# Routed blocks of the second feed-forward as three products of rounded parts, with the parts of the weights made in the first

## The chip, the core and the metric

The kernel runs on one core of a Trainium2 chip. The metric is the time of one execution on the device, in microseconds (us); lower is better. Several executions are timed and their median is given; one more is recorded by the hardware profiler. The core has five engines with an instruction stream each: PE (TensorE, the matrix array, fed by a sequencer of its own), DVE (VectorE), ACT (ScalarE), POOL (GpSimd) and SP (SyncE, which here only starts transfers). They wait for each other through semaphores.

## The reference

```python
def _layernorm(x, axis=-1, eps=1e-05): ...
x = L0_attn_x                                   # 8 x 512 x 256 float32
x = x + 0.5 * ffn(_layernorm(x), ...)
x = x + attention(_layernorm(x), ...)           # 16 heads of 16, causal
x = x + 0.5 * ffn(_layernorm(x), ...)           # same weights as the first

def ffn(x, router_w, expert_bias, shared_w1, shared_w2, shared_w3, routed_w1, routed_w2, routed_w3):
    shared_out = silu(x @ shared_w1) * (x @ shared_w2) @ shared_w3      # hidden width 1024
    scores = sigmoid(x @ router_w)                                      # 16 experts
    _, top_idx = top_k(scores + expert_bias, 2)
    gates = scores of the two chosen experts, 0 for the others
    for each expert e:                                                  # hidden width 256
        acc = acc + silu(x @ routed_w1[e]) * (x @ routed_w2[e]) @ routed_w3[e] * gates[:, e]
    return shared_out + acc
```

All is float32. The bias makes the choice of experts uneven. Running this reference's own arithmetic on its inputs gives, for the second feed-forward, these 128-row blocks for each of the 16 experts in turn: 26, 3, 27, 1, 2, 0, 0, 3, 0, 0, 0, 0, 4, 0, 2, 0 (68 blocks with rows in them).

## The kernel before

The stages follow one another: `norm_first`, `feed_forward` (tag f1_), `attention`, `feed_forward` (tag f2_). The same function serves both feed-forwards; the argument `fill` is true for the first alone.

**The shared part.** 4096 rows are taken in 8 chunks of 512. Five chunks (`BEHIND` = 5) run before the routed blocks (`chunks_before`) and three after (`chunks_behind`). Here each float32 operand is already kept as a rounded high part and a low part (type float32r), and a product is three matmuls of parts: high by high, high by low, low by high (lines 943, 959, 963). Meanwhile DVE works out the routing, SP loads the 16 experts' weights (`load_expert`, tile f_ew: ew12 and ew3), and POOL scatters the rows into `rows_by_slot`, sorted by expert into 128-row blocks.

**The routed blocks.** There are always NB = 80 blocks, each with one expert; `bexp_i` holds the expert's number of each, and blocks beyond the last used one take expert 15. `steps` lets every engine walk through steps i = 0 to 81; in step i PE (function `step` under `block.tensor`) does this in order: read the number of block i's expert from SBUF into a register (`value_load`, L998), two plain float32 matmuls 128x512 with that expert's w1 and w2 (L1007), the two transposes of the hidden rows of block i-1 (L1015), the two transposes of the input rows of block i+1 (`turn_x`, L994), read the expert's number of block i-2 again, and its two float32 matmuls 128x256 with w3 (L1028). Weight addresses depend on the register, so each matmul with an expert's weights needs one address instruction on PE's sequencer (FUSED_REGOPS). ACT copies the turned input out of PSUM (L654) and takes silu (L647); DVE multiplies (L897), copies the turned hidden rows (L894) and the result (L904); POOL scatters the result to `outputs_by_choice` (L612); SP fetches the next block's rows, four blocks ahead (L491). The loop is rolled: 4 steps written out, 6 turns of 12, then 6 more steps.

The order on each engine is the order in which the code is written. A wait on PE's sequencer holds everything written behind it on PE.

Of the kernel before, what the change touches and what calls it, by code (L numbers as in the profile page):

```python
# [6 lines left out]
P = 128  # L7
F32 = mybir.dt.float32
# [8 lines left out]
CT = 4  # L17
# [26 lines left out]
class Mem:  # L44
# [8 lines left out]
    def ps(self, name, shape, dt=F32):  # L53
        return self.ctx.enter_context(self.nc.psum_tensor(self.tag + name, shape, dt))

# [224 lines left out]
def feed_forward(nc, z, g, dram, tag, x_src, fill, out):  # L280
# [11 lines left out]
    BEHIND = NC - 3  # L292
    with ExitStack() as ctx:  # L293
        m = Mem(nc, ctx, tag)
        ew12 = m.sb("ew12", [P, E, KD, 2 * RH])
        ew3 = m.sb("ew3", [P, E, KR, z.D])
        ewf = ew12[:].rearrange("p e k n -> p (e k n)")
# [15 lines left out]
        rawx = m.sb("rawx", [P, KD, CHUNK])  # L313
        xparts = m.sb("xparts", [P, 2, 2, KD, CHUNK], F32R)
        xr = m.sb("xr", [P, 2, CT, z.D])
        sil = m.sb("sil", [P, 2, CHUNK])
        hid = m.sb("hid", [P, 2, CHUNK])
        hparts = m.sb("hparts", [P, 2, 2, CHUNK], F32R)
# [8 lines left out]
        bexp_i = m.sb("bexp_i", [1, NB], I32)  # L327
# [3 lines left out]
        xq = m.sb("xq", [P, 4, CT // 2, z.D])  # L331

        bcmp = early([NB, E])[0:1]

# [3 lines left out]
        far0 = E * KD * 2 * RH - 2 * (IN_A + IN_B) - 4 * NT * TOPK - 2 * NB  # L338
        assert used[0] <= far0
        far_experts = E - -(-(E * KD * 2 * RH - far0) // (KD * 2 * RH))  # L340
# [14 lines left out]
        yr = xq[:, 0:2].rearrange("p u t d -> p (u t) d")  # L355
        assert used[0] <= E * KD * 2 * RH and KD * CHUNK == 4 * z.D and CHUNK == 2 * RH
# [58 lines left out]
        mid = m.sem("mid")  # L415
        summed = m.sem("summed")
# [8 lines left out]
        def steps(eng, body):  # L425

            for r in range(4):
                body(0, r, lambda lag, n=r: 0 <= n - lag < NB)

            assert (NB // 4 - 2) % 3 == 0  # L430
            with eng.Fori(0, (NB // 4 - 2) // 3) as turn:
                for part in range(3):
                    for r in range(4):
                        body(turn * 3 + (part + 1), r, lambda lag: True)
            for n in range(NB - 4, LAST + 1):
                body(n // 4, n % 4, lambda lag, n=n: 0 <= n - lag < NB)
# [17 lines left out]
        def _(sp):  # L454
# [28 lines left out]
            def load_expert(e):  # L483
                for dst, src in ((ew12[:, e, :, 0:RH], dram.routed_w1), (ew12[:, e, :, RH:], dram.routed_w2),
                                 (ew3[:, e], dram.routed_w3)):
                    sp.dma_start(dst, src[e].rearrange("(k p) n -> p k n", p=P)).then_inc(ew_in, 16)

# [24 lines left out]
            store(BEHIND - 1, (BEHIND - 1) % 2)  # L512
            with sp.Fori(0, NB // 4 - 1) as q:
                for r in range(4):
                    fetch(q + 1, r)
# [101 lines left out]
        def _(act):  # L617
# [25 lines left out]
            def step(q, r, has):  # L643
# [4 lines left out]
                if has(-1):  # L648
                    evacuate(i + 1, (r + 1) % 2)

# [5 lines left out]
            evacuate(0, 0)  # L656
            steps(act, step)
# [3 lines left out]
        def _(dve):  # L661
# [54 lines left out]
            def expert_blocks():  # L716

                link(v.tensor_scalar(small[:, 0, :], upto[:, :, NT - 1], float(P - 1), None, ALU.add))
# [59 lines left out]
            def block_experts():  # L778
# [6 lines left out]
                link(v.tensor_copy(bexp_i[:], bexp[:]))  # L785
# [100 lines left out]
            dve.sem_inc(hT_ev, 1)  # L886
# [3 lines left out]
            def step(q, r, has):  # L890
                i = q * 4 + r
                if has(1):
# [18 lines left out]
        def _(pe):  # L911
# [85 lines left out]
            def expert(i):  # L997
                return pe.value_load(bexp_i[0:1, bass.ds(i, 1)], min_val=0, max_val=E - 1)  # L998
# [894 lines left out]
```

## Time and profile before

| | us |
|---|---|
| median of 3 runs | 1705.95 |
| the 3 runs | 1703.82, 1705.95, 1710.88 |
| profiled execution, its time | 1703.97 |
| profiled execution, span from first to last instruction | 1702.0 |
| shared part of the first feed-forward, from 60 to 261 us | 201 |
| routed blocks of the first, 261 to 505 | 244 |
| its last three chunks, 505 to 615 | 110 |
| attention, 615 to 1140 | 525 |
| shared part of the second, 1140 to 1349 | 209 |
| routed blocks of the second, 1349 to 1592 | 243 |
| its last three chunks, 1592 to 1702 | 110 |

The profile gives for each engine its busy time, for groups of instructions their mean duration and what ended the idle time before them. PE shows as two rows: PE for matmuls and PEld for weight loads. The instructions that PE's sequencer executes itself (register loads, address arithmetic, semaphore waits) are marked PEldq and count as busy nowhere. PEclk is the granted clock, 1.00 being the higher of its two levels.

### The profile page before, as it was taken

How to read it: one execution, taken by the hardware profiler on the slowest of the kernel's cores; microseconds unless marked ns; L12 is line 12 of the kernel's file. 1: busy time of each engine (PE TensorE's matmuls, PEld its weight loads, DVE VectorE, ACT ScalarE, POOL GpSimd, SP SyncE). 2: the span in 40 equal slices, each digit the busy share in tenths (PEclk: the TensorE clock that was granted, in tenths of full speed). 3: DMA queues.
4: the chain of work that ended last, by engine and by line, in shares of the span. 5: the costliest groups of instructions: out<-in, count | busy, mean ns of one | idle time of the engine just before them, and what ended most of it. 6: DMA issues, size and time to landing. Idle time of an engine off the chain costs nothing. (4 is left out here: it accounts for less than half of the span.)

```text
span 1702.0 us, 27697 instructions
## 1 busy us (share of the span) xinstructions
PE 1552.6 (91%) x8388; PEld 1138.9 (67%) x8389; DVE 886.3 (52%) x1844; ACT 583.8 (34%) x1110; POOL 590.4 (35%) x832
## 2 busy tenths in 40 slices
PE   6699999999999948989998999856999999999998
PEld 5688885666668835556665666535888766666787
DVE  5377633333336637666565666515775333333466
ACT  1322222222223224545554555514222222222232
POOL 3328812333330043453454353422377033333200
PEclk9999999999999978999998999867999999999999
DMA  7678832222237334344444344124196322222661
GB/s 235 212 268 286 288 122 76 88 87 87 87 127 239 101 109 106 87 113 110 129 123 112 97 118 125 61 75 161 62 341 225 103 88 87 88 87 86 196 209 50
DMA packets 176951, 231.88 MB, mean 136 GB/s; under 512 B 20162, under 2 KB 136386, under 8 KB 176850
## 3 DMA queue, kind: packets, MB, share of 16 engines
q1 hardware_dynamic: 157746, 173.94, 34.1%
q0 software_dynamic: 19104, 56.64, 9.4%
q8 instruction: 57, 0.93, 0.2%
q14 instruction: 44, 0.36, 0.1%
HBM read 117.47 MB, written 83.10 MB: 118 GB/s over the span
## 5 line engine op out<-in xcount | busy, mean ns | idle before, releaser
L943 PE MATMUL f_bank<-f_xparts,f_sw 128*128 128x512 f32 x1536 | 382.9, 399 | 23.4 <-DVE f_sw L881 21.0
L943 PEld LDWEIGHTS f_bank<-f_xparts,f_sw 128*128 128x128 f32 x1536 | 286.5, 193 | 80.9 <-issue 25.1
L1007 PE MATMUL f_bank<-f_ew,f_hid 128*128 x640 | 302.4, 595 | 3.5 <-ACT f_hid L654 3.5
L612 POOL DMA_INDIRECT outputs_by_choice<-f_xq,f_home x160 | 153.2, 957 | 424.8 <-DVE f_xq L904 402.1
L1571 DVE TENSOR_REDUCE at_mx<-at_ps 128x1 f32<-128x384 f32 (+3 forms) x352 | 212.6, 632 | 102.4 <-PE at_ps L1700 101.5
L1484 ACT ACTIVATE at_pT<-at_ps 128x512 f32<-128x512 f32 (+1 forms) x352 | 194.9, 560 | 87.1 <-PE at_ps L1716 77.0
L1401 POOL TENSOR_SCALAR_AFFINE_SELECT at_pT<-at_pT 128x128 f32<-128x128 f32 (+2 forms) x352 | 121.4, 347 | 255.9 <-ACT at_pT L1484 253.8
L894 DVE COPY f_hid<-f_bank 128x256 f32<-128x256 f32 x160 | 68.0, 425 | 242.5 <-PE f_bank L1015 242.5
L647 ACT ACTIVATE f_sil<-f_bank 128x256 f32<-128x256 f32 x160 | 61.5, 384 | 351.8 <-PE f_bank L1007 349.6
L580 POOL DMA_INDIRECT rows_by_slot<-f_xq,slot x128 | 141.2, 1103 | 110.3 <-DVEq L741 71.9
L1007 PEld LDWEIGHTS f_bank<-f_ew,f_hid 128*128 128x128 f32 x640 | 114.2, 189 | 97.4 <-issue 89.0
L1716 PE MATMUL at_ps<-at_qT,at_kT 98*128 98x256 f32 (+3 forms) x512 | 172.6, 389 | 4.1 <-DMA at_qT<-at_mT 2.2
L1028 PE MATMUL f_bank<-f_ew,f_hid 128*128 x640 | 164.9, 380 | 0.8 <-DVE f_xq L904 0.8
L636 ACT CAST f_hparts<-f_hid 128x512 fp32r<-128x512 f32 x128 | 79.3, 620 | 240.3 <-DVE f_hid L833 224.0
L1696 PE MATMUL at_ps<-at_kT,at_qT 96*128 96x512 f32 (+2 forms) x384 | 148.8, 404 | 7.7 <-DMA at_qT<-at_loT 6.2
L959 PEld LDWEIGHTS f_bank<-f_sw,f_hparts 128*128 128x128 f32 x1024 | 139.2, 191 | 23.5 <-ACT f_hparts L636 7.2
L833 DVE TENSOR_TENSOR f_hid<-f_sil,f_bank 128x512 f32<-128x512 f32 x128 | 87.9, 687 | 126.5 <-PE f_bank L943 94.2
L959 PE MATMUL f_bank<-f_sw,f_hparts 128*128 128x256 f32 x1024 | 144.9, 284 | 9.7 <-ACT f_hparts L636 4.4
L835 DVE TENSOR_TENSOR f_hparts<-f_hid,f_hparts 128x512 fp32r<-128x512 f32 x128 | 92.2, 720 | 87.8 <-ACT f_hparts L636 76.1
L634 ACT ACTIVATE f_sil<-f_bank 128x512 f32<-128x512 f32 x128 | 76.5, 597 | 157.0 <-PE f_bank L943 132.9
L1028 PEld LDWEIGHTS f_bank<-f_ew,f_hid 128*128 128x128 f32 x640 | 109.1, 190 | 10.2 <-issue 1.9
L1015 PEld LDWEIGHTS f_bank<-ident,f_sil 128*128 128x128 f32 x320 | 44.9, 141 | 84.1 <-issue 83.3
(160 smaller groups left out, 1968.7 us busy)
## 6 DMA issues: line engine op xcount, KB each, us to landing
f_ew<-in_L_ffn_routed_w_dram SPq DMA_DIRECT2D x96, 256.0 KB
f_rawx<-rows_by_slot SPq DMA_DIRECT2D x160, 128.0 KB, 1.9
f_ew<-outputs_by_choice SPq DMA_DIRECT2D x16, 1024.0 KB, 6.8
rows_by_slot<-zero POOLq DMA_DIRECT2D x10, 1024.0 KB, 18.5
f_rawx<-xn_turned SPq DMA_DIRECT2D x16, 512.0 KB
f_xq<-xn_rows POOLq DMA_DIRECT2D x32, 256.0 KB
at_qT<-at_hiT SPq DMA_DIRECT2D x64, 128.0 KB, 2.8
at_kT<-at_hiT SPq DMA_DIRECT2D x128, 64.0 KB, 2.7
```

Source lines behind the costliest of these rows:

```text
L580: nc.gpsimd.indirect_dma_start(dram.xs, bass.IndirectOffsetOnAxis(ap=g.slot[:, at:at + 1], axis=0), xq[:, h % 4, t, :], None).then_inc(sca ...
L612: nc.gpsimd.indirect_dma_start(dram.yk, bass.IndirectOffsetOnAxis(ap=home[:, i:i + 1], axis=0), yr[:, i % 4, :], None).then_inc(y_st[i % 4 ...
L835: v.tensor_tensor(hparts[:, j % 2, 1], hid[:, j % 2], hparts[:, j % 2, 0], ALU.subtract).then_inc(h_lo, 1)
L943: ins = pe.matmul(ps[j % 2][:, :], sw12[:, wp, k, w, j * P:(j + 1) * P], xparts[:, u, xp, k, :], start=(i == 0), stop=(i == 3 * KD - 1))
L959: pe.matmul(psO[t], hparts[:, j % 2, 0, t * P:(t + 1) * P], sw3[:, wp, j, :], start=(j == 0 and wp == 0 and t % 2 == 0), stop=False, skip_ ...
L1007: ins = pe.matmul(rUp[r % 2][:, :], xsT[:, r % 2, k * P:(k + 1) * P], w12[:, bass.ds(e * (KD * 2 * RH) + k * 2 * RH, 2 * RH)], start=(k == ...
L1028: ins = pe.matmul(rY[r % 2][:, 0:z.D], hrT[:, r % 2, k * P:(k + 1) * P], w3[:, bass.ds(e * (KR * z.D) + k * z.D, z.D)], start=(k == 0), st ...
L1401: p.affine_select(out=own, in_=own, compare_op=ALU.is_ge, fill=0.0, base=0, pattern=[[0, heads], [1, P]], channel_multiplier=-1).then_inc( ...
L1484: s_.activation(pT[:, i % SLOTS, 0:w], ps2[i % RING2][:, 0:w], ACT.Exp).then_inc(ex_done, 1)
L1571: v.tensor_reduce(own, ps1[i % RING1][:, 0:heads * w].rearrange("p (j a x) -> p j a x", a=min(heads, 2), x=w), AX.X, ALU.max).then_inc(mx_ ...
L1696: pe.matmul(ps[:, j * w:(j + each) * w], qT[0:ROWS, G % KEEP, (h + j) // 2, qi * P:w], kT[0:ROWS, G % KEEP, h + j:h + j + each, 0:w], star ...
L1716: ins = pe.matmul(ps[:, j * w:(j + 1) * w], kT[0:LAST_ROWS, G % KEEP, h + j, ki * P:(ki + 1) * P], qT[0:LAST_ROWS, G % KEEP, (h + j) // 2, ...
```

## The change

In the first feed-forward (`exact` = False) the routed blocks compute as before. Beside them, ACT copies each expert's weights rounded (high part) into a staging tile and DVE subtracts to get the low part, an expert for every four blocks from block 4 on; SP stores both parts, 1.5 MB for an expert, to a new DRAM tensor `wparts`. In the second (`exact` = True) the 16 high parts are loaded into SBUF (one transfer an expert in place of three), while the low parts go into a ring of four experts, refilled by SP as the blocks of an expert are done. A routed product is three float32r matmuls of parts for each half of the contraction, six in place of two. The rows are split where they are turned: ACT copies the high part and DVE subtracts, for the input and for the hidden rows. PE's steps are written out without a loop; a step reads three values for each block (a count for the wait on the ring, the offset of the high part, the offset in the ring) once, and keeps them for the second product. Every expert now gets at least one block, so block counts become 26, 3, 27, 1, 2, 1, 1, 3, 1, 1, 1, 1, 4, 1, 2, 1 (76), and blocks 75 to 79 have expert 15. The fetch of rows in the second feed-forward moves from SP to ACT.

```diff
@@ feed_forward
+    W12, W3 = KD * 2 * RH, KR * z.D
+    EW, RING = W12 + W3, 4
+    exact = not fill
...
-        def steps(eng, body):
-            for r in range(4):
-                body(0, r, lambda lag, n=r: 0 <= n - lag < NB)
...
+        def steps(eng, body, unrolled=False):
+            Q = 2 + (E - 2 if not unrolled else 0)
+            for n in range(8):
+                body(n // 4, n % 4, lambda lag, n=n: 0 <= n - lag < NB, n // 4 % 2)
+            if not unrolled:
+                with eng.Fori(0, (E - 2) // 2) as turn:
+                    for part in range(2):
+                        for r in range(4):
+                            body(turn * 2 + (part + 2), r, lambda lag: True, part)
+            for n in range(Q * 4, LAST + 1):
+                body(n // 4, n % 4, lambda lag, n=n: 0 <= n - lag < NB, n // 4 % 2)
@@ SP
+            def load_low(e):
+                s = 3 * e % RING
+                sp.dma_start(ring[:, s * EW:(s + 1) * EW].bitcast(F32), dram.wparts[e * P:(e + 1) * P, EW:]
+                             ).then_inc(lo_ld[s], 16)
+            def low_in(e):
+                sp.wait_ge(lo_ld[3 * e % RING], 16 * (e // RING + 1))
+                sp.sem_inc(lo_ready, 1)
...
+                for e in range(RING, E):
+                    end = sp.value_load(ends_i[0:1, e - RING:e - RING + 1], min_val=1, max_val=NB)
+                    sp.wait_ge(dn_done, end)
+                    load_low(e)
+                    low_in(e)
...
+                        sp.dma_start(dram.wparts[bass.ds(e * P, P), :], stage[:, u].bitcast(F32).rearrange("p h n -> p (h n)")
+                                     ).then_inc(part_st, 16)
@@ ACT
+                if r < 2 and e is not None:
+                    lo, hi = ((0, W12), (W12, EW))[r]
...
+                    nc.scalar.copy(stage[:, u, 0, lo:hi], ewf[:, bass.ds(e * EW + lo, hi - lo)]).then_inc(hi_made, 1)
+            def step_exact(q, r, has, u):
+                i = q * 4 + r
+                if has(-1):
+                    high_x(i + 1, (r + 1) % 2)
+                if has(-4):
+                    nc.scalar.dma_start(xs[:, r], dram.xs[bass.ds(q * (4 * P) + (4 + r) * P, P), :]
+                                        ).then_inc(xs_ld[r], 16)
...
+                    nc.scalar.copy(hrP[:, (r - 1) % 2, 0], rTh[:, 0:KR * P]).then_inc(hT_hi, 1)
@@ DVE
+                link(v.tensor_scalar(small[:, 0, :], upto[:, :, NT - 1], float(P - 1), float(P), ALU.add, ALU.max))
...
+                if has(-1) and exact:
+                    low_rows(i + 1, (r + 1) % 2)
...
+                    v.tensor_tensor(hrP[:, (r - 1) % 2, 1], rTh[:, 0:KR * P], hrP[:, (r - 1) % 2, 0], ALU.subtract
+                                    ).then_inc(hT_lo, 1)
...
+                    v.tensor_tensor(stage[:, u, 1, lo:hi], ewf[:, bass.ds(e * EW + lo, hi - lo)], stage[:, u, 0, lo:hi],
+                                    ALU.subtract).then_inc(lo_made, 1)
@@ PE
+            def step_exact(q, r, has, u):
+                i = q * 4 + r
+                if has(-1):
+                    turn_x((i + 1) // 4, (i + 1) % 4)
+                if has(0):
+                    at[i] = [pe.value_load(bexp_i[0:1, n, i:i + 1], min_val=0, max_val=(E, (E - 1) * EW, (RING - 1) * EW)[n])
+                             for n in range(3)]
+                    pe.wait_ge(xT_lo, i + 1)
+                    pe.wait_ge(rh_done, i + 1)
+                    n = 0
+                    for xp, w, base in ((0, whi, at[i][1]), (1, whi, at[i][1]), (0, ring, at[i][2])):
+                        if w is ring:
+                            pe.wait_ge(lo_ready, at[i][0])
+                        for k in range(KD):
+                            ins = pe.matmul(rUp[r % 2][:, :], xsP[:, r % 2, xp, k * P:(k + 1) * P],
+                                            w[:, bass.ds(base + k * 2 * RH, 2 * RH)],
+                                            start=(n == 0), stop=(n == 3 * KD - 1))
...
```

In the order listings, a row is one instruction or several alike; ISA is an instruction of the sequencer itself (address arithmetic or check), TENSOR_LOAD a read of one value into a register. Semaphore names of the first feed-forward stand in some rows of the second because the numbers are used again.

PE, second feed-forward, one step among the last six of the blocks before: f_hid holds the turned rows, f_bexp_i the experts' numbers, f_sil the hidden rows, f_rawx the fetched rows. Behind these rows stand the two matmuls of the second product (L1028), each with an ISA row ahead.

```order
L998 TENSOR_LOAD f_bexp_i
L998 ISA x2
L1007 ISA [waits f2_rh_done,f2_xT_ev]
L1007 MATMUL f_bank<-f_ew,f_hid 128x512
L1007 ISA
L1007 MATMUL f_bank<-f_ew,f_hid 128x512
L1015 MATMUL f_bank<-ident,f_sil 128x128 [waits f2_hT_ev,f2_rh_done]
L1015 MATMUL f_bank<-ident,f_sil 128x128
L994 MATMUL f_bank<-ident,f_rawx 128x128 [waits f2_xT_ev,f2_xs_ld1]
L994 MATMUL f_bank<-ident,f_rawx 128x128
L998 TENSOR_LOAD f_bexp_i
L998 ISA x2
```

PE, second feed-forward, the same part of a step in the changed kernel, behind the turning of the next input (L1153), which has moved to the step's head: f_both is the tile that now holds the tables, f_hparts the turned rows in parts, f_whi and f_ring the weights.

```order
L1166 TENSOR_LOAD f_both
L1166 ISA x2
L1166 TENSOR_LOAD f_both
L1166 ISA x2
L1166 TENSOR_LOAD f_both
L1166 ISA x2
L1175 ISA [waits f2_rh_done,f2_xT_lo]
L1175 MATMUL f_bank<-f_whi,f_hparts 128x512
L1175 ISA
L1175 MATMUL f_bank<-f_whi,f_hparts 128x512 x3
L1175 ISA [waits f2_lo_ready]
L1175 MATMUL f_bank<-f_ring,f_hparts 128x512
```

Register reads are three in a row where there was one in each half of the step; a product has four ISA rows of addresses and six matmuls where it had two and two. One more ISA row and one more matmul of L1175 follow; the second product (L1194) has the same form and no read of its own.

SP, second feed-forward, behind the last of the five chunks: the refills of the ring in the changed kernel. In the kernel before, the fetches of rows stood here.

```order
L533 DMA f_ring<-weights_in_parts 128x1536 [waits f2_lo_ld3,f2_lo_ld2,f1_y_ld3,f1_th_done]
L582 TENSOR_LOAD f_both [waits f2_lo_ld1]
L582 ISA x2
L533 DMA f_ring<-weights_in_parts 128x1536 [waits f2_dn_done]
L582 TENSOR_LOAD f_both [waits f2_lo_ld0]
```

Each refill waits for the one before it to have landed and for the blocks of the expert that it replaces.

## Rows read from the trace of the kernel before

**Rows 1.** Stages: length, busy time by engine (x instructions), clock, DMA share, GB/s.

```profile
615.00:1140.00 525.00, 452.88 (x3048) 302.75 (x3048) 299.16 (x625) 263.79 (x489) 226.88 (x456) 0.90 0.40 107
...
1349.00:1592.00 243.00, 241.28 (x951) 147.75 (x952) 92.61 (x237) 60.43 (x160) 73.71 (x77) 1.00 0.28 87
```

**Rows 2.** Timeline of PE in the second feed-forward's blocks: start us, duration us, line, count.

```profile
1582.86 1.88 PE L1007 MATMUL f_bank<-f_ew,f_hid 128*128 x4
1584.58 0.38 PE L1015 MATMUL f_bank<-ident,f_sil 128*128 128x128 f32 x2
1584.80 0.38 PE L994 MATMUL f_bank<-ident,f_rawx 128*128 128x128 f32 x2
1585.01 1.03 PE L1028 MATMUL f_bank<-f_ew,f_hid 128*128 x4
```

**Rows 3.** PE's sequencer, line by line, same stretch: ns min/median/max, first and last start.

```profile
L1007 PEldq FUSED_REGOPS  x3: 46/46/46, 1582.6 to 1585.6; - x3
...
L1013 PEldq EVENT_SEMAPHORE  x1: 51/51/51, 1582.9 to 1582.9; - x1
...
L992 PEldq EVENT_SEMAPHORE  x1: 51/51/51, 1583.0 to 1583.0; - x1
...
L998 PEldq TENSOR_LOAD <-f_bexp_i x2: 296/298/301, 1583.1 to 1584.1; - x2
L998 PEldq FUSED_REGOPS  x2: 151/151/151, 1583.5 to 1584.5; - x2
L998 PEldq SEQ_ASSERT  x2: 18/18/18, 1583.7 to 1584.7; - x2
...
L1026 PEldq EVENT_SEMAPHORE  x1: 51/51/51, 1583.8 to 1583.8; - x1
...
L1028 PEldq FUSED_REGOPS  x2: 46/46/46, 1583.9 to 1584.0; - x2
...
L1005 PEldq EVENT_SEMAPHORE  x1: 51/51/51, 1584.8 to 1584.8; - x1
```

**Rows 4.** Line 998 over the whole execution.

```profile
L998 PEldq TENSOR_LOAD <-f_bexp_i x320: 296/302/892, 260.5 to 1592.8; - x160
```

**Rows 5.** Timeline of PE in the second feed-forward's shared part.

```profile
1337.39 2.91 PE L943 MATMUL f_bank<-f_xparts,f_sw 128*128 128x512 f32 x12
1340.14 1.11 PE L959 MATMUL f_bank<-f_sw,f_hparts 128*128 128x256 f32 x8
...
1341.57 0.40 PE L943 MATMUL f_bank<-f_xparts,f_sw 128*128 128x512 f32 x1
```

**Rows 6.** Groups by shape, 1340 to 1600 us: busy us, mean ns, idle time before.

```profile
L897 DVE TENSOR_TENSOR f_sil<-f_sil,f_bank 128x256 f32<-128x256 f32 x80 | 32.8, 410 | 3.5 <-ACT f_sil L647 3.5
...
L654 ACT COPY f_hid<-f_bank 128x256 f32<-128x256 f32 x80 | 29.8, 373 | 9.0 <-PE f_bank L994 3.6
```

**Rows 7.** Timelines of PE at the start and the end of those blocks.

```profile
1349.01 0.44 PE L994 MATMUL f_bank<-ident,f_rawx 128*128 128x128 f32 x2 [1.34 <-DVE f_xr L799]
1350.00 1.55 PE L1007 MATMUL f_bank<-f_ew,f_hid 128*128 x3 [0.55 <-ACT f_hid L654]
...
1595.62 0.70 PE L943 MATMUL f_bank<-f_xparts,f_sw 128*128 128x512 f32 x2 [0.78 <-issue]
```

**Rows 8.** DMA issues: KB each, median us from issue to landing.

```profile
f_rawx<-rows_by_slot SPq DMA_DIRECT2D x160, 128.0 KB, 1.9
f_ew<-outputs_by_choice SPq DMA_DIRECT2D x16, 1024.0 KB, 6.8
...
xn_turned<-nf_xnT SPq DMA_DIRECT2D x8, 512.0 KB, 3.4
```

**Rows 9.** Lines 627 and 881, and DVE's timeline in the first feed-forward's blocks.

```profile
L627 ACT CAST f_sw<-f_ew x12: 1044/1046/1057, 66.3 to 1165.0; 128x1024 fp32r<-128x1024 f32 x12
...
L881 DVE TENSOR_TENSOR f_sw<-f_ew,f_sw x4: 1225/1226/1226, 67.4 to 1160.4; 128x1024 fp32r<-128x1024 f32 x4
...
402.81 0.42 DVE L894 COPY f_hid<-f_bank 128x256 f32<-128x256 f32 x1 [1.51 <-PE f_bank L1015]
```

More of the change, by code:

```diff
@@ L54, in ps, with over @@
         return self.ctx.enter_context(self.nc.psum_tensor(self.tag + name, shape, dt))
+    def over(self, name, shape, dt=F32):
+        with self.nc.sbuf_tensor(self.tag + name, shape, dt) as at:
+            return at
     def sem(self, name):
@@ L511, in _, with step @@
                 fetch(0, r)
[L512 to L515, printed above, removed]
+            last = BEHIND - 1
+            if exact:
+                sp.wait_ge(h_lo, BEHIND * z.JS - 1)
+                load_low(0)
+                sp.wait_ge(b_done, BEHIND * z.JS)
+                load_low(1)
+                sp.wait_ge(sh_st[1 - last % 2], 16 * (BEHIND // 2))
+                load_low(2)
+                low_in(0)
+                store(last, last % 2)
+                low_in(1)
+                low_in(2)
+                sp.wait_ge(sh_st[last % 2], 16 * (last // 2 + 1))
+                sp.wait_ge(h_lo, BEHIND * z.JS)
+                load_low(3)
+                low_in(3)
+                for e in range(RING, E):
[3 more added lines that the diff above has]
+                    low_in(e)
+            else:
+                store(last, last % 2)
+                sp.sem_inc(part_free, 1)
+                def step(q, r, has, u):
+                    if has(-4):
+                        fetch(q + 1, r)
+                    e = parted(q)
+                    if r == 3 and e is not None:
+                        if not isinstance(e, int) or e > 0:
+                            sp.wait_ge(part_st, e * 16)
+                            sp.sem_inc(part_free, 1)
+                        sp.wait_ge(lo_made, e * 2 + 2)
+                        sp.sem_inc(g.held, 1)
+                        sp.dma_start(dram.wparts[bass.ds(e * P, P), :], stage[:, u].bitcast(F32).rearrange("p h n -> p (h n)")
+                                     ).then_inc(part_st, 16)
+                steps(sp, step)
+                sp.wait_ge(part_st, 16 * E)
+                sp.sem_inc(part_free, 1)
             sp.wait_ge(tx_done, NB + 4)
@@ L641, in _, with step @@
             act.sem_inc(xT_ev, 1)
-            def step(q, r, has):
+            def step(q, r, has, u):
                 i = q * 4 + r
@@ L984, in _ @@
             pe.wait_ge(sh_done, BEHIND * CT + 4)
[L985 to L987 removed]
+            pe.wait_ge(ew_in, 16 * E if exact else 3 * 16 * E)
             def turn_x(q, r):
@@ L1001, in step @@
+            def step(q, r, has, u):
                 i = q * 4 + r
```

178 lines of the change are left out of this document (138 added, 40 removed).

## The prediction, made before the changed kernel was run

> **What bounds the kernel now.** I read the table of stages first. The routed blocks of the second feed-forward take 243 us, PE is busy for 241.3 of them at granted clock 1.00, DVE for 93, ACT for 60 [rows 1]. So this stage is bound by PE, and what the change is worth there is read from PE's step. Next, PE's timeline: one step is two products that start at 1582.86, two transposes at 1584.58, two at 1584.80 and the second product at 1585.01 [rows 2]. The first product so takes 1.72 us, the transposes 0.43, and the step, from one sequencer instruction of line 1007 to its like (1582.6 to 1585.6), 3.02 us [rows 3], with no gap. Then I read what this timeline leaves out: PE's sequencer, which must issue the work. It is not idle. From 1582.6 it goes through address instructions, waits and two register reads until 1584.8, where it has reached the next product's wait and stands until 1585.6 [rows 3]. So it works about 2.2 us of 3.02. The array sets the step now; the sequencer is 0.8 us behind it.
>
> **What the array does after the change.** The shared part already runs products of parts. Twelve matmuls of 512 columns take 1337.39 to 1340.14, 0.229 us each; twelve of 256 take until 1341.57, 0.119 each [rows 5]. A changed step has six of each and the same four transposes: 6 x 0.229 + 6 x 0.119 + 0.43 = 1.37 + 0.71 + 0.43 = 2.52 us. Taken alone, the array saves 0.50 us a step, 40 us over the stage. That is the gain on offer.
>
> **What the sequencer does after the change.** Two prices come from its rows [rows 3]. A register read is a TENSOR_LOAD (0.30 us), an address check (0.15) and an assertion (0.02), strictly one after another with pauses between. From its start to the next instruction passes 0.6 to 0.7 us (1583.1 to 1583.8, and 1584.1 to 1584.8, printed to a tenth); I take 0.66. The other instructions, semaphore waits and address arithmetic (each with the array instructions that it precedes), follow each other in 0.10 to 0.13 us: four between 1582.6 and 1583.1, three between 1583.8 and 1584.1; I take 0.115. Test on the old step: 2 x 0.66 + 7 x 0.115 = 2.13, against 2.2 read.
> A changed step has three reads in place of two. Of the small instructions there are four that carry or are waits (head of the step, first product, hidden transposes, second product) and eight of address arithmetic, four for each product, in place of four: 12. Hence 3 x 0.66 + 12 x 0.115 = 1.98 + 1.38 = 3.36 us. This is more than the array's 2.52 and more than the old 3.02. The bound changes hands: **the sequencer sets the step, at 3.36 us**. It reads far ahead only if it is faster than the array; here it is slower, so running ahead gives nothing. From both sides: with 0.62 and 0.10 the step is 3.06, with 0.70 and 0.13 it is 3.66. I take the middle since it reproduces the old step. The third read and the doubled addresses are thus the price, (3.36 - 3.02) x 79 steps = **+26.9 us**, and the array stands idle 0.84 us in each step.
>
> The Trainium skill (DMA: Bandwidth & Descriptors, Latency and other measured facts) puts the floor of a `tensor_load` at about 600 ns. The median here is 302 ns over 320 reads [rows 4], so the trace disagrees and I go by it; an estimate with the page's floor would add 0.30 us to each of three reads, a step of 4.26 us.
>
> **ACT and DVE.** Each step now has on ACT two copies of high parts (0.37 each as line 654) and silu, and on DVE two subtractions, a product and the result's copy (each about 0.41 as line 897) [rows 6]: 1.1 and 1.7 us of 3.36. The input is turned a whole step ahead. They hide under the sequencer's step; if it were 2.52 they would still fit. The row fetches, now issued by ACT, sit behind a copy that is not urgent.
>
> **Start and end.** Before, the first transposes start at 1349.01 and the first product at 1350.00 [rows 7]. Now a copy and a subtraction (0.41 more) stand before the second turning, and then three reads (1.98) before the first product; its wait for the first copy alone ended at about 1349.9, so the product starts near 1352.6: **+2.6 us**. At the end a subtraction more stands before the last product: **+0.5 us**.
>
> **The ring.** With the block counts given, experts 0 to 3 are in the ring from the start, and the short experts follow each other in blocks 56 to 75. A refill brings 768 KB. Landing times [rows 8]: 128 KB 1.9 us, 1024 KB 6.8, 512 KB 3.4; along either line 768 KB take 4.4 to 5.4 us. Refills are serial on SP, and between two stand SP's own register read and the issue (0.9 us), so one takes 5.3 to 6.3. Expert 6's refill can begin when block 55 has passed its second product, at step 58.4; expert 12 is wanted at step 68.8. That is seven refills, 37 to 44 us, in 10.4 steps of 3.36 = 35 us: a stall of 2 to 9 us. The short end is nearer, since refills with 6 KB rows meet little other traffic (DMA share 0.28, 87 GB/s [rows 1]): **+2 us**. A wait there holds the whole of PE's stream behind it.
>
> **The first feed-forward.** Its blocks have the old matmuls and 16 experts' parts beside them. The rounding copy of 1024 columns costs ACT 1.05 us and the subtraction DVE 1.23 [rows 9]. DVE is idle 1.51 us in the step shown before line 894 [rows 9], and ACT has 243 - 60 us free [rows 1]; both fit in a gap, none is behind PE's next wait. If the cover were gone it would be 16 x 1.2 = 19 us. Each store is 1.5 MB; along the same landing line it takes 8 to 10 us, stands on SP's queue ahead of a fetch that is needed 12 us later, and comes once in 12 us. Hidden, 0 us. The loop's new form costs nothing where steps have no gap.
>
> **The second shared part.** Expert loads become 16 transfers in place of 48, 12.6 MB as before; PE waits for none of them. Eight small DVE operations more lie beside PE's 200 us. 0 us.
>
> **Sum.** 1703.97 + 26.9 + 2.6 + 0.5 + 2 = 1736.0 for the profiled execution; it lies 2 us under the median 1705.95, so 1738.
>
> **Rivals.**
> *The array sets the step.* If a register read did not hold the stream (if reads overlap each other and the array's queue stays full), the step is 2.52: -0.50 x 79 = -39.5, +3.1 for start and end. The ring then hurts more: 10.4 steps are 26 us against refills of 37 to 44, a stall of 11 to 18, say 14. 1704 - 39.5 + 3.1 + 14 + 2 = 1684. This is the case on the other side; it decides where the sequencer's step falls under 3.02, and wins fully under 2.52. For it: array instructions cost the sequencer nearly nothing, and the reads come in a row. Against it: in each of the two reads seen, check and assertion start only after the load has ended [rows 3]. Chance 0.13. A half-way case, small instructions at 0.08 and reads at 0.6, gives 2.76 to 3.0 and a time of 1695 to 1712: 0.06.
> *Reads take longer.* The longest of the 320 took 0.89 us [rows 4], against 0.30. If three in a row met each other's latency and took 0.60 each, the step were 4.26 and the time 1738 + 71 = 1809. (In the Trainium skill, DMA: Bandwidth & Descriptors, the floor quoted above would give the same.) Nothing in a typical step speaks for it: 0.03.
> *The stores disturb the first feed-forward.* The fetch is issued 3 us after the store and wanted 12 us later; if a store took 19 us, it would land some 6 us late, 16 times, 96 us in all. It needs half the speed that every landing row shows: 0.02.
> *The clock falls.* PE would be busy 75% of each step. Attention has it busy 453 of 525 us and a mean clock of 0.90, but blocks 1.00 [rows 1]. At half clock the array's step is 5.0 us, +160 us. The gaps are under 1 us: 0.02.
> *The change does not do what it says* (the parts are no faster): excluded by rows 5.
>
> **How the numbers follow.** The forecast has 0.74, between 1714 (step 3.06, no stall) and 1768 (3.66 and a stall of 9 would be 1769). With most of the half-way case, and without the tip of the forecast's long end, the range is 1700 to 1764; 0.2 is left out, most of it on the array's side. What a measurement can tell from no change is 0.5%, 8.5 us, 1697 to 1714. Slower by more: the forecast and the three rivals behind it, 0.80. Faster: the array's case and the fast end of the half-way one, 0.14. Within: the rest of that, 0.06.
>
> **What would show it.** In the changed profile: the second blocks stage about 272 us with PE busy near 75%; the sequencer's rows without a standing wait, three loads 0.65 us apart; matmuls of 512 and 256 columns in runs of six at 0.229 and 0.119; a hole of 0.8 us ahead of each first product; a few waits for the ring at blocks 60 to 68; the first feed-forward's blocks still 3.02 a step. I am wrong if the stage is shorter than 243 us, or if a step has a different length than three loads and twelve small instructions give.

## The result and the profile after the change

The changed kernel takes 1770.78 us (median of 4 runs, 1770.22 to 1772.36), the kernel before 1707.05 on the same chip (1703.82 to 1710.88): a ratio of 1.0374, interval 1.035 to 1.0397. The forecast was slower, by 32 us; it is 64, and 1770.78 lies above the range of 1700 to 1764. The profiled span grew by 68.6 us, from 1702.0 to 1770.6.

Stages after, in the columns of [rows 1]: the first feed-forward's blocks, the second shared part, the second blocks, the tail.

```profile
255.00:517.00 262.00, 246.21 (x958) 148.30 (x956) 121.86 (x273) 83.84 (x192) 75.81 (x77) 1.00 0.50 177
...
1155.00:1366.00 211.00, 188.41 (x1050) 163.05 (x1050) 123.02 (x199) 64.38 (x97) 96.00 (x87) 0.93 0.53 187
1366.00:1664.00 298.00, 228.92 (x1280) 185.45 (x1280) 121.76 (x322) 81.78 (x240) 75.02 (x78) 0.98 0.36 116
1664.00:1770.00 106.00, 100.77 (x576) 88.64 (x576) 64.26 (x126) 31.08 (x50) 1.93 (x2) 1.00 0.45 148
```

PE is no longer the bound in the second blocks: busy 229 us of 298, where it was 241 of 243. For every kernel below I measure a blocks stage from the first to the last start of the line of the first product, since this does not depend on where a window is cut. The rows of the kernel after, second blocks (L1175, two groups, since the third product reads the ring) and first blocks (L1207); columns: ns min/median/max, first and last start.

```profile
L1175 PE MATMUL f_bank<-f_whi,f_hparts x320: 387/395/791, 1370.7 to 1658.9; 128*128 x160
L1175 PE MATMUL f_bank<-f_ring,f_hparts x160: 387/392/675, 1372.6 to 1659.3; 128*128 x160
```

```profile
L1207 PE MATMUL f_bank<-f_ew,f_hid x320: 592/592/692, 258.1 to 514.9; 128*128 x160
```

Before, line 1007 ran from 1350.0 to 1590.2 and from 261.6 to 501.8, 240.2 us each. So the second blocks went from 240.2 to 288.6 (+48.4) and the first ones from 240.2 to 256.8 (+16.6). The other differences are small: work ahead of the first blocks -3.5, attention with what lies around it +0.1, the second shared part +4.4 (first to last start 188.1 against 183.7), the gap in front of the second blocks +3.1, their end -0.5, the tail 0. The sum is 68.6. Two terms carry the miss of 36 us in the profiled execution: the second blocks, 19.5 more than the step and the ring were given, and the first ones, 16.6 where the prediction had 0.

**A step of the second blocks.** PE's timeline, as in [rows 2]:

```profile
1384.54 1.18 PE L1175 MATMUL f_bank<-f_whi,f_hparts 128*128 x4 [0.86 <-DVE f_hparts L1058]
1385.56 0.62 PE L1175 MATMUL f_bank<-f_ring,f_hparts 128*128 x2
1386.02 0.38 PE L1185 MATMUL f_bank<-ident,f_sil 128*128 128x128 f32 x2
1386.16 0.71 PE L1194 MATMUL f_bank<-f_whi,f_hparts 128*128 x4
1386.71 0.40 PE L1194 MATMUL f_bank<-f_ring,f_hparts 128*128 x2
1386.95 0.38 PE L1153 MATMUL f_bank<-ident,f_rawx 128*128 128x128 f32 x2
1388.09 1.19 PE L1175 MATMUL f_bank<-f_whi,f_hparts 128*128 x4 [0.76 <-issue]
```

Here the work of the array starts at 1384.54 and ends at 1387.33, and a hole of 0.76 us stands before the next product. Such holes have two names in the list of PE's waits (1378 to 1660; total us, times, longest):

```profile
PE f_bank L1175 <- issue: 40.0, 52, 0.9
PE f_bank L1175 <- DVE f_hparts L1058: 21.5, 23, 1.2
PE f_bank L1175 <- SPq L538: 1.6, 1, 1.6
```

The 21.5 us look like waits for DVE's subtraction of line 1058. They are not. Here are the sequencer's own rows over one step, 1443.4 to 1447.0. The last line is the next step's first read:

```profile
L1166 PEldq TENSOR_LOAD <-f_both x3: 300/306/518, 1443.4 to 1444.9; - x3
L1166 PEldq FUSED_REGOPS  x3: 146/151/151, 1443.8 to 1445.3; - x3
L1166 PEldq SEQ_ASSERT  x3: 18/18/18, 1444.0 to 1445.5; - x3
L1169 PEldq EVENT_SEMAPHORE  x1: 51/51/51, 1445.6 to 1445.6; - x1
L1175 PEldq FUSED_REGOPS  x4: 42/46/51, 1445.7 to 1446.1; - x4
L1183 PEldq EVENT_SEMAPHORE  x1: 51/51/51, 1446.2 to 1446.2; - x1
L1190 PEldq EVENT_SEMAPHORE  x1: 51/51/51, 1446.3 to 1446.3; - x1
L1194 PEldq FUSED_REGOPS  x4: 46/46/46, 1446.4 to 1446.8; - x4
L1151 PEldq EVENT_SEMAPHORE  x1: 51/51/51, 1446.9 to 1446.9; - x1
...
L1166 PEldq TENSOR_LOAD <-f_both x1: 303/303/303, 1447.0 to 1447.0; - x1
```

Here no instruction stands. Three reads start at 1443.4, 1444.1 and 1444.9 and are done at 1445.6 (2.2 us); then the wait of 1169, four instructions of line 1175, the waits of 1183 and 1190, four of 1194 and the wait of 1151 follow, 1445.6 to 1447.0, about 0.12 us each. In [rows 3] the sequencer arrived at the next product's wait early and stood. The hole ahead of this step is one of those called issue, so one step does not settle the 23 others. The whole stage does: from the wait of 1169 to the first instruction of 1175 pass 0.106 us (median) and 0.265 at most in the 77 steps recorded from 1378 to 1660, so that PE never stood for DVE there. The semaphore named in the list of waits is only the last one that had been passed. The step is three reads and twelve small instructions, as forecast, but both are longer: 0.12 for 0.115, and one of the reads took 518 ns where [rows 4] have a median of 302. Over the stage the step's median is 3.61 us. The only long stand of the sequencer from 1378 on is one for the ring, in the step of 1616.

**The first blocks**, which I had put at nothing, have a long step in four. PE's timeline around one:

```profile
374.50 1.88 PE L1207 MATMUL f_bank<-f_ew,f_hid 128*128 x4
...
376.65 1.03 PE L1228 MATMUL f_bank<-f_ew,f_hid 128*128 x4
378.39 1.98 PE L1207 MATMUL f_bank<-f_ew,f_hid 128*128 x4 [0.71 <-issue]
```

The DMA share and the GB/s (last two columns) in that microsecond, and the two reads of PE's sequencer that fall into the steps of 374 and 377 (the second row groups three reads, 1163 ns is the longest):

```profile
375.00:376.00 1.00, 1.00 (x4) 0.45 (x3) 0.12 (x1) 0.00 (x0) 0.00 (x0) 1.00 1.01 393
```

```profile
L1157 PEldq TENSOR_LOAD <-f_both x1: 910/910/910, 374.8 to 374.8; - x1
...
L1157 PEldq TENSOR_LOAD <-f_both x3: 300/302/1163, 376.6 to 380.0; - x3
```

All sixteen DMA engines are busy with the store of one expert's parts (1.5 MB), and a register read out of SBUF takes 0.91 and 1.16 us in place of 0.30. 34 of the 160 reads of these blocks are over 0.6 us.

### The profile page after: what moved, and what is told of

It reads as the page before. It is cut to its first block and busy times, and to the rows that moved or that the text cites. A ratio compares the mean times of both kernels' runs of the same rounds, so it can differ in the third digit from the quotient of the medians.

```text
span 1770.6 us, 28709 instructions
## 1 busy us (share of the span) xinstructions
PE 1542.8 (87%) x8708; PEld 1175.9 (66%) x8709; DVE 942.1 (53%) x1964; ACT 628.5 (35%) x1222; POOL 593.0 (33%) x832
## 3 DMA queue, kind: packets, MB, share of 16 engines
q8 instruction: 72, 1.18, 0.3%
## 5 line engine op out<-in xcount | busy, mean ns | idle before, releaser
L701 POOL DMA_INDIRECT outputs_by_choice<-f_yr,f_home x160 | 155.6, 973 | 488.4 <-DVE f_yr L1046 421.4
L1207 PE MATMUL f_bank<-f_ew,f_hid 128*128 x320 | 152.6, 599 | 14.5 <-issue 12.7
L1035 DVE TENSOR_TENSOR f_sil<-f_sil,f_bank 128x256 f32<-128x256 f32 x160 | 66.5, 415 | 170.7 <-ACT f_sil L759 167.2
L1175 PE MATMUL f_bank<-f_whi,f_hparts 128*128 x320 | 97.0, 425 | 64.7 <-issue 42.4
L1175 PEld LDWEIGHTS f_bank<-f_whi,f_hparts 128*128 128x128 f32 x320 | 56.6, 191 | 88.9 <-issue 83.2
L1207 PEld LDWEIGHTS f_bank<-f_ew,f_hid 128*128 128x128 f32 x320 | 57.1, 189 | 65.4 <-issue 61.1
L1922 PEld LDWEIGHTS at_ps<-at_qT,at_kT 98*128 98x128 f32 x512 | 90.1, 202 | 8.5 <-ACT at_pT L1690 4.2
L1030 DVE COPY f_hid<-f_bank 128x256 f32<-128x256 f32 x80 | 34.0, 424 | 110.3 <-PE f_bank L1215 109.3
## 6 DMA issues: line engine op xcount, KB each, us to landing
f_ew<-in_L_ffn_routed_w_dram SPq DMA_DIRECT2D x48, 256.0 KB
```

The source lines that it names most:

```text
L701: nc.gpsimd.indirect_dma_start(dram.yk, bass.IndirectOffsetOnAxis(ap=home[:, i:i + 1], axis=0), yr[:, i % 4, :], None).then_inc(y_st[i % 4 ...
L1175: ins = pe.matmul(rUp[r % 2][:, :], xsP[:, r % 2, xp, k * P:(k + 1) * P], w[:, bass.ds(base + k * 2 * RH, 2 * RH)], start=(n == 0), stop=( ...
L1207: ins = pe.matmul(rUp[r % 2][:, :], xsT[:, r % 2, k * P:(k + 1) * P], ewf[:, bass.ds(e * EW + k * 2 * RH, 2 * RH)], start=(k == 0), stop=( ...
L1922: ins = pe.matmul(ps[:, j * w:(j + 1) * w], kT[0:LAST_ROWS, G % KEEP, h + j, ki * P:(ki + 1) * P], qT[0:LAST_ROWS, G % KEEP, (h + j) // 2, ...
```

## The experiments

They divide into what sets a step of the second blocks, what disturbs the first ones, and the ring. Stage lengths are measured as above. The kernel before took 1702 to 1717 us on the chips of these runs, so a total is compared only with before on the same chip, and the argument goes by the stages of the profiles. A total without a range was measured once.

**Is it the number of reads?** In `one_read` the two addresses are computed from the number in place of being read.

```diff
-                    at[i] = [pe.value_load(bexp_i[0:1, n, i:i + 1], ...) for n in range(3)]
+                    e = pe.value_load(bexp_i[0:1, 0, i:i + 1], min_val=1, max_val=E)
+                    at[i] = [e, (e - 1) * EW, ((e * 3 - 3) & (RING - 1)) * EW]
```

> The changed kernel, but in the second feed-forward PE reads one value a block; the other two numbers are worked out from it in registers (2 or 3 small instructions). Theory A (PE's sequencer sets the step, 3.61 us = 3 reads and 12 small instructions): two reads of about 0.70 us go and about 0.3 us of small instructions comes, step 2.5 to 2.7 us, the stage 210 us in place of 289, the ring costs 5 to 15 us instead of 2; time about 1695 to 1705. Theory B (the chain of ACT's copy and DVE's subtraction, which the waits name 23 times before the first product, sets it): step stays near 3.6, time stays at 1770.

Measured: 1703.49 us, before on that chip 1716.54, ratio 0.9934 (0.9902 to 0.9965), so 0.7% under before. Second blocks 1375.6 to 1589.4, 213.8 us in place of 288.6. PE's timeline:

```profile
1401.23 1.17 PE L1175 MATMUL f_bank<-f_whi,f_hparts 128*128 x4
1402.24 0.63 PE L1175 MATMUL f_bank<-f_ring,f_hparts 128*128 x2
1402.70 0.38 PE L1185 MATMUL f_bank<-ident,f_sil 128*128 128x128 f32 x2
1402.84 0.72 PE L1194 MATMUL f_bank<-f_whi,f_hparts 128*128 x4
1403.39 0.40 PE L1194 MATMUL f_bank<-f_ring,f_hparts 128*128 x2
1403.63 0.39 PE L1153 MATMUL f_bank<-ident,f_rawx 128*128 128x128 f32 x2
1403.77 0.48 PE L1175 MATMUL f_bank<-f_whi,f_hparts 128*128 x1
```

1401.23 to 1403.77 is 2.54 us without a hole: the array's step, forecast as 2.52. The same work with two reads fewer is 1.07 us a step faster, and then the array sets it.

`fixed_addresses` has no read at all; every block of the second feed-forward takes the parts of one expert from the resident weights, so the output is another.

```diff
-                    at[i] = [pe.value_load(...) for n in range(3)]
+                    at[i] = [E if i == NB - 1 else 1, 0, 0]
...
-                    for xp, w, base in ((0, whi, at[i][1]), (1, whi, at[i][1]), (0, ring, at[i][2])):
+                    for xp, w, base in ((0, whi, at[i][1]), (1, whi, at[i][1]), (0, whi, at[i][2])):
...
```

> Part of the work is changed: in the second feed-forward every block uses one expert's high parts at a fixed address for all three products, so PE reads nothing, does no address arithmetic, and waits for the ring only at the start and at the last block. Theory A: the array sets the step, 2.52 us as the sum of its rows, stage about 200 us. Theory B: step stays near 3.6 us.

Measured: 1691.39 us; second blocks 1371.4 to 1572.6, 201.2 us, each step 2.54. One read more or less no longer moves the step. What one_read has on top, 12.6 us, lies almost whole in five steps, those of blocks 61 and 66 to 69: the ring.

`two_reads` computes only the ring's address.

```diff
+                    e, hi_at = [pe.value_load(bexp_i[0:1, n, i:i + 1], ...) for n in range(2)]
+                    at[i] = [e, hi_at, ((e * 3 - 3) & (RING - 1)) * EW]
```

> The changed kernel with two values read for each block in the second feed-forward in place of three (the ring's offset is worked out in registers). Theory A: 3.61 less one stretched read (0.70 to 0.78) plus 2 or 3 small instructions of 0.125: a step of 3.1 to 3.25 us, between the three reads' 3.61 and the one read's 2.54. A theory by which one read already is the bound of something else would give 2.54 or 3.61.

Measured: 1724.09 us against 1702.09 for before on that chip; second blocks 1362.1 to 1611.1, 249.0 us, median step 3.03 us. PE's timeline:

```profile
1401.72 1.20 PE L1176 MATMUL f_bank<-f_whi,f_hparts 128*128 x4 [0.17 <-issue]
```

The step is a little shorter than the 3.1 to 3.25 expected. With 0, 1, 2 and 3 reads it is 2.54, 2.54, 3.03 and 3.61: flat under the array, then +0.49 and +0.58. These differences are not the price of a read alone: two_reads has fourteen small instructions where the kernel after has twelve, and its second read is seldom stretched (mean 319 ns; see below).

**Why 3.61 and not 3.36?** In `no_scatter` GpSimd leaves out the scatters of the second blocks' results, so that these never arrive.

```diff
                 if i >= 2:
                     pool.wait_ge(y_st[(i - 2) % 4], 16 * ((i - 2) // 4 + 1))
                     pool.sem_inc(y_free, 1)
+                if exact:
+                    pool.sem_inc(y_st[i % 4], 16)
+                    continue
```

> Part of the work is left out: POOL's scatter of the routed results in the second feed-forward (the semaphores are raised without it). Theory E (the second of the three reads, mean 0.43 us against 0.30, is stretched while the scatter's transfer reads SBUF): all three reads 0.30, step 3.61 - 0.13 = about 3.48 us. Rival: the stretch comes from the row fetch on ACT's queue or from ACT and DVE themselves, and the second read stays at 0.43.

Measured: 1752.61 us; second blocks 1361.8 to 1639.6, 277.8 us, median step 3.46. The reads of the second blocks, in the kernel after and in this one (ns min/median/max):

```profile
L1166 PEldq TENSOR_LOAD <-f_both x240: 295/302/752, 1368.1 to 1657.2; - x120
```

```profile
L1169 PEldq TENSOR_LOAD <-f_both x239: 293/299/319, 1360.3 to 1637.5; - x120
```

The long reads are gone, 319 ns is the longest. In the kernel after it is the second read of a step that stretches (mean 427 ns; the first 308, the third 299): it falls beside the scatter. In the kernel after, the reads over 0.4 us had 32 packets of the scatter's queue under way beside them on average, those under 0.31 us three. This is 0.15 us of the 0.25 a step, 11 us in all. The other 0.10 remains without the scatter: the twelve small instructions take 1.52 us a step on average in both kernels, 0.126 each rather than 0.115, and the three reads 1.96 without the scatter, where 1.98 was forecast.

**How far was the old step from the sequencer?** `before_plus_one` and `before_plus_two` are the kernel before with one or two reads more, whose value nobody uses, ahead of the second product's, in both feed-forwards.

```diff
+                    expert(i - 2)
+                    expert(i - 2)
                     e = expert(i - 2)
```

> The kernel before with one more register read in each step of both feed-forwards' blocks (three in place of two; its value is not used). Theory A: the sequencer had 0.75 us in hand in a step written out and some 0.1 to 0.3 less in the loop, a read costs 0.64; step 3.02 to 3.2 us, 0 to 25 us over 160 steps. A theory by which a read costs its full time wherever it stands would give 3.66 and +100 us.

> The kernel before with two more register reads a step. Theory A: 1.28 us of reads against 0.45 to 0.75 in hand, step 3.55 to 3.85 us, +85 to +130 us. A theory by which reads hide behind the array's work whatever their number gives 3.02.

Measured: 1749.6 and 1852.32 us, against 1704.45. The second blocks:

```profile
L1007 PE MATMUL f_bank<-f_ew,f_hid x320: 592/592/692, 1375.6 to 1634.3; 128*128 x160
```

```profile
L1007 PE MATMUL f_bank<-f_ew,f_hid x320: 592/592/692, 1427.9 to 1735.9; 128*128 x160
```

258.7 and 308.0 us for 240.2: per step +0.23 for the first read and +0.62 for the second. The second one pays in full, the first one all but the slack that there was; so the old sequencer had 0.62 - 0.23 = 0.4 us in hand, not the 0.8 of the prediction. Both expectations were too low for this reason (+45 us measured for up to 25, +148 for 85 to 130; the two blocks stages together have 37 and 135 of these, and the rest, spread over the other stages, was not traced). The 0.8 came from [rows 3], a step of the end that is written out. In the rolled part of the kernel before each read has an address instruction of its own (42 ns) ahead of it, beside the check (151 ns), and one register instruction more stands at line 1004:

```profile
L998 PEldq FUSED_REGOPS  x4: 42/96/151, 1400.3 to 1402.7; - x4
L1004 PEldq ALU_OP  x1: 32/32/32, 1400.7 to 1400.7; - x1
```

Three instructions of about 0.1 us each are the difference. The trace of the kernel before has it directly: between the wait of line 1005 and the first instruction of line 1007 the sequencer stood 0.74 us in each of the last three steps, which are written out, and 0.45 us on average over the steps of either stage.

**What disturbs the first blocks?** `no_store` stores only the first expert's parts, and every load of parts takes that one (the output is another); all rounding work stays.

```diff
...
+                        if isinstance(e, int) and e == 0:
                             sp.dma_start(dram.wparts[0:P, :], stage[:, u] ...)
```

> Part of the work is left out: 15 of the 16 stores of weight parts in the first feed-forward; the second loads the first expert's parts 16 times. The copies and subtractions stay. Theory C (a bulk store stretches PE's register reads from 0.30 to about 1.0 us, and that makes one step in four 3.9 to 4.2 us long): steps of the first feed-forward's blocks are all 3.02, its blocks 17 us shorter than in the changed kernel (257 us), near 240. Rival D (ACT's copy of 1024 columns holds the next step): no difference, one step in four stays near 4 us.

Measured: 1762.39 us; first blocks 258.2 to 501.1, 242.9 us. Two steps are long: the first of the stage (4.44 us, in which the granted clock fell to 0.5) and one of 4.05 us behind the one store that is left. All others take 3.02. PE's timeline at the place shown above:

```profile
374.93 1.03 PE L1229 MATMUL f_bank<-f_ew,f_hid 128*128 x4
375.80 1.88 PE L1208 MATMUL f_bank<-f_ew,f_hid 128*128 x4
...
378.81 1.88 PE L1208 MATMUL f_bank<-f_ew,f_hid 128*128 x4
```

So ACT's and DVE's rounding work is hidden, as the prediction had it, and the fifteen stores left out cost at least 13.9 us. The second blocks, where this edit and the next two change nothing that PE does, took 287.1, 287.7 and 287.5 us in these kernels: their +48 repeats.

`keep_number` leaves the stores and takes reads away: within a body of eight steps of the first blocks the number read for the first product is kept in a register for the second one (96 reads for 160).

```diff
-                    e = expert(i - 2)
+                    e = kept.pop(place[0] - 2, None)
+                    if e is None:
+                        e = expert(i - 2)
```

> The changed kernel, but in the first feed-forward PE keeps the number read for a block's first product for its second, where the code is one body; reads fall from 160 to about 100, and the stores stay. Theory C: the sequencer has 1.3 us in hand where it had 0.75, and one read in place of two falls under a store, so the stretched steps shrink by 0.5 to 1.0 us, blocks 243 to 250 us. Rival D: no difference, 257 us.

Measured: 1759.91 us; first blocks 260.0 to 508.2, 248.2 us; seven long steps, each eighth, in place of sixteen, where a body starts and two reads are still made.

`split_only` keeps the reads and sends the 1.5 MB as three smaller stores in the three steps in which their pieces become ready.

```diff
-                    if r == 3 and e is not None:
+                    if r in (1, 2, 3) and e is not None:
...
+                        sp.dma_start(to[:, h, c], stage[:, u, h, c] ...).then_inc(part_st, 16)
```

> The changed kernel with each store of weight parts cut into three in successive steps, and nothing else. Theory C: a burst of 1.4 us meets one read, rarely two, stretch 0.7 against 0.75 in hand; the first feed-forward's blocks take 241 to 248 us in place of 257, so cutting alone gives most of it. If it needs the kept number too, they stay above 250.

Measured: 1773.71 us against 1704.45; first blocks 260.7 to 512.3, 251.6 us, above the range of 241 to 248 expected. A smaller store still stretches reads (30 long ones for 34), but only six steps are more than 0.5 us too long: most of a smaller stretch falls into slack. Each remedy alone gets a part back, of 16.6 us 8.6 and 5.2.

**All remedies.** `one_read_kept_split` joins one_read, keep_number and split_only.

> One read a block in the second feed-forward; in the first, the number kept for the second product, and each expert's store cut into three (512, 512 and 512 KB) in successive steps. Theory C: a burst is over in 1.4 us and meets at most one read, so it costs less than the sequencer has in hand; the first feed-forward's blocks take 240 to 243 us in place of 257. Time 15 us under the run with one read alone. If the number of bytes and not the length of a burst mattered, it would stay at 257.

Measured: 1682.46 us (1681.5 to 1686.78), ratio to before 0.9889 (0.9846 to 0.9933). First blocks 256.0 to 499.0, 243.0 us, no step over 3.3 us though 34 of its 96 reads are still over 0.6: with one read a step the sequencer has room for them. Against one_read the first blocks are 13.9 us shorter (15 expected). Second blocks 213.5 us, of which the array's steps are 201.2. Of the 12.3 us on top the wait list, 1360 to 1568, names 7.8:

```profile
PE f_bank L1183 <- SPq L538: 7.8, 4, 2.8
```

The granted clock adds to this. Behind the longest of these waits it was 0.50, which the list does not show. Four matmuls that take 1.17 us elsewhere take 2.05, and the step, which waits for nothing, 3.66 us in place of 2.54:

```profile
1513.67 0.73 PE L1183 MATMUL f_bank<-f_ring,f_hparts 128*128 x2 [2.79 <-SPq L538]
...
1515.76 2.05 PE L1183 MATMUL f_bank<-f_whi,f_hparts 128*128 x4
```

```profile
1515.00:1518.00 3.00, 3.00 (x11) 2.55 (x10) 1.46 (x4) 0.46 (x2) 0.96 (x1) 0.50 0.86 282
```

Each step with a wait is also some 0.6 us longer than its wait and 2.54 us together. Behind a wait the sequencer, which had stood, comes late: from the first matmul behind the wait at 1529.06 to the next product at 1531.09 it works without a stand, 2.03 us, where the array alone takes 1.53. The waits themselves are the ring: SP starts an expert's refill only when it has seen the one before land. `ring_two_in_flight` waits for a refill only after it has issued the next one.

```diff
                     load_low(e)
-                    low_in(e)
+                    if e > RING:
+                        low_in(e - 1)
+                low_in(E - 1)
```

> The kernel with one read, kept numbers and split stores, and SP issues the refill of the next expert before it waits for the last one to land. With one read the ring costs about 12 us in steps 62 to 70 (4.9, 5.8, 4.5, 6.1 and 3.3 us in place of 2.54). If serial refills are the cause, at most 3 us remain, and the time is 8 to 10 us under the run without it. If the bandwidth or the wait for finished blocks is the cause, nothing changes.

Measured: 1676.37 us (1667.26 to 1679.53), ratio 0.9833 (0.9795 to 0.9871): 1.7% under the kernel before, and 6 us under one_read_kept_split, where 8 to 10 were expected. Second blocks 1353.5 to 1563.4, 209.9 us; the same line of the wait list:

```profile
PE f_bank L1185 <- SPq L538: 3.1, 2, 2.0
```

4.7 us of waiting are gone, but only 3.6 of the 12.3 us of the stage; 8.7 stay above the array's steps. So serial refills were a part of the ring's price and not all of it. With two refills in flight each one takes longer to land, 6.0 us (median) in place of 4.7. How much of the 8.7 us this explains was not tested.

## Why the prediction was right in direction and short in size

Two terms failed: the price of the sequencer's step was too low (19.5 us short), and the first feed-forward was put at nothing because its work was covered (16.6 us). With only one of the two the time would have stayed inside the range.

- **What bounds, and who takes over**: right. PE set the step before, its array would need 2.52 us after (2.54 measured without the reads), its sequencer more. The series 0 to 3 reads shows this; the list of waits alone would have blamed DVE for a third of it.
- **The step, 3.36 us, +26.9**: a term that failed in its size, right in form. It measured 3.61, within the bounds 3.06 to 3.66, and the stage +48.4 where step and ring together had +28.9. Of the 19.5 us between, no_scatter shows 11 as stretched reads; some 8 us (0.10 x 79) are the price of the small instructions, 0.126 us each for 0.115. The test on the old step (2.13 against 2.2) had shown that the prices came out low; I took the midpoint anyway.
- **"The sequencer is 0.8 us behind it"**: wrong, 0.4 us over the stage (before_plus_one and _two), 0.74 only where the steps are written out. It changed nothing in the second blocks, which are written out, but in the first ones it did.
- **The first feed-forward, 0 us**: the reasoning that failed, +16.6. I looked for cover on ACT, DVE and SP's queue, found it, and no_store shows that it was there. I did not ask what a store of 1.5 MB does to PE's reads, though [rows 4] held one of 892 ns. Two long reads add 0.61 + 0.86 us to a sequencer with 0.4 us of slack: 1.1 us lost, and sixteen steps of 3.7 to 4.2 us in place of 3.02 are 15.6 of the 16.6. The rival on the stores named the right cause with the wrong victim (the row fetch).
- **Start, +2.6**: +3.1. A copy, a subtraction and three reads ahead of the first product, as said:

```profile
1366.63 0.44 PE L1153 MATMUL f_bank<-ident,f_rawx 128*128 128x128 f32 x2 [1.34 <-DVE f_xr L934]
1368.09 0.41 PE L1153 MATMUL f_bank<-ident,f_rawx 128*128 128x128 f32 x2 [1.01 <-DVE f_hparts L1058]
1370.71 2.07 PE L1175 MATMUL f_bank<-f_whi,f_hparts 128*128 x4 [2.22 <-issue]
```

- **End, +0.5**: -0.5. The subtraction stands there (two waits of 0.42 and 0.21 for line 1039), but the wait of 0.41 us for the copy of a result (DVE, line 904), which stood ahead of the last products before, is gone, and so is part of each product's time: six matmuls take 0.96 to 0.99 us where four took 1.03 and more.
- **The ring, +2**: right. One wait, in a step of 5.95 us, and a refill landing in 4.6 us (forecast 4.4 to 5.4):

```profile
1616.02 1.18 PE L1175 MATMUL f_bank<-f_whi,f_hparts 128*128 x4 [0.97 <-DVE f_hparts L1058]
1618.76 1.10 PE L1175 MATMUL f_bank<-f_ring,f_hparts 128*128 x2 [1.55 <-SPq L538]
```

  With the array's step it costs 12 us (one_read against fixed_addresses), where the rival had 14. The rival took all of it for waiting; about 8 are waits.
- **The second shared part, 0**: +4.4 in the profile, not settled. PE's work there is the same in all kernels. It took 183.7 to 184.7 us in the three of before's form and 183.8 to 188.8 in the ten of the changed form; ring_two_in_flight, which makes the same loads as the kernel after, has 183.8. So the new loads don't cost it by themselves, and what does stays open. So does the -3.5 ahead of the first blocks.
- **Reads take longer (1809)**: its price was that all three reads take 0.60 us. That did not come; one in three took 0.43. The Trainium skill's floor of about 600 ns for a `tensor_load` (DMA: Bandwidth & Descriptors, Latency and other measured facts) is not seen here either: the median of the second blocks' reads is 299 to 303 ns in every run that has them.
- **Array (1684), half-way, clock**: none came. The granted clock was 0.50 in the first two steps (2.07 us for four matmuls that take 1.18) and once more from 1619 to 1622, behind the ring's wait; the steps of 3.61 us hid this one, and the mean is 0.98. Under the array's shorter step such a fall costs time, as one_read_kept_split showed.
- **The range**, 1700 to 1764, left no room for three losses together, the reads beside the scatter (11 us), the small instructions (8) and the reads beside the stores (16.6): its bounds of the step covered the first two, and the first feed-forward had no bound but "hidden". Its lower end has a slip as well: a step of 3.06 without a stall of the ring gives 1712, not 1714.

## What to carry to other kernels

Add up the sequencer of an engine as you would the engine: so many register reads by 0.65 us and small instructions by 0.12 to 0.13, and compare this with the array's step before you make the array faster; a value that two others follow from by a shift or a product is read once. If a loop holds such reads, its slack is that of the rolled step, and a bulk transfer put beside it is priced by what it does to the reads, also where every engine's own work is covered. Where refills of a ring are serial, issuing the next one before waiting for the last helps, but expect a part only: here it gave 3.6 of 12.3 us, and each refill took longer. A wait can also cost what no list of waits shows, a lower clock behind it.

## What the runs showed of the hardware

- A register read out of SBUF takes 0.30 us (median), 0.65 with its check and assertion (1.96 us for three in no_scatter). In the rows the next read starts only behind the assertion of the last, and one more in a step that the sequencer sets adds 0.62 us (before_plus_one to before_plus_two).
- Such a read is stretched by transfers. Beside a 1.5 MB store that holds the DMA share at 1.01 (393 GB/s) it takes 0.91 to 1.16 us; beside a scatter from SBUF 0.43 on average (second read of a step; 319 ns at most in no_scatter).
- Address arithmetic and semaphore waits on PE's sequencer follow each other at 0.126 us (1.52 us for twelve, kernel after and no_scatter).
- Six matmuls of 512 and six of 256 columns on rounded parts, with four transposes, take 2.54 us in a row, in fixed_addresses in every step behind the first few, and with one read ahead of them (one_read) in nearly all that do not wait for the ring.
- Behind a wait of 2.79 us the granted clock was 0.50 from 1515 to 1518 us (one_read_kept_split), behind one of 1.55 us from 1619 to 1622 (kernel after).
